# Mixing each tile with four row-tiled products on TensorE instead of one product with a masked block matrix

## The chip, the cores and the metric

The kernel runs on one core of one Trainium2 chip. Its metric is the device time of one execution in microseconds, the median of several executions. A profile is one further execution; its span runs from the first to the last instruction and is shorter than its time, which also has what lies around the instructions.

## The reference

`x` has 64 batches of 32 channels by 512 features. Two layers are applied and the result is added to `x`:

```python
W = weights[condition]                       # (64, 32, 32), one of 16 matrices for each batch
y = einsum('bct,bcd->bdt', x, W)             # mixes the 32 channels of a batch
result = einsum('bnd,od->bno', y, W_base) + b_base
logits = einsum('bnd,ed->bne', y, W_gate)    # 8 experts
route_w = top-2 of softmax(logits), divided by their sum, 0 elsewhere
h = einsum('bnd,erd->bner', y, A)            # rank 16 for each expert
delta = einsum('bner,eor->bno', h * route_w[..., None], B)
out = x + result + delta
```

All of it is float32. The large products are done as three products of values split into a high and a low part (`hi*hi + hi*lo + lo*hi`, type float32r); the mixing is a plain float32 product.

## The kernel before

**Tiles.** A tile is four batches (Q = 4), 4 x 32 channels on the 128 partitions, by 512 features; there are 16 tiles. `x_sb[:, t, :]` holds tile t, `mixw[:, t, :]` the four 32x32 mixing matrices of its batches, one below the other (partition = batch in tile x 32 + channel). The first two tiles' matrices are picked out of a table by TensorE, the other 14 are gathered by indirect DMAs of GpSimd.

**Mixing.** VectorE (`select`, L366) multiplies `mixw` with a mask, `diag_mask`, so that a 128x128 block-diagonal matrix `mix[t % 2]` arises. TensorE (`mix_tile`, L508) then makes y transposed, features on the partitions: for each of 4 chunks of 128 features one product with `x_sb[:, t, chunk]` (128x128) as the stationary operand and `mix` (128 columns) as the moving one, into one PSUM bank `y_ps[t % 2]`. A float32 product is two pairs of weight load and matmul in the trace, so a tile has 8 pairs. Tile 0's second half goes into another bank (`hwT_ps[0]`), so that its first half can be read early.

**The rest of a tile.** ScalarE makes `y_hi` (`split_y`, L287) and VectorE `y_lo` (`low_y`, L382), both two-buffered. TensorE's `main_step` (L521) runs 12 steps (4 chunks, 3 products of split values), two matmuls each, into the two banks of `main_ps[t % 2]`: base sums, LoRA ranks and gate logits. VectorE routes (`route_tile`: the top two, weights, `hw`), TensorE transposes `hw` (`turn`, L531) into the bank `hwT_ps[t % 2]`, ScalarE and VectorE split it (`split_hwT` L298, `low_hwT` L416), and `lora` (L537) adds six matmuls to the base sums. VectorE adds the bias and the sums to x (`add_bias` L423, `finish` L427), and SyncE stores.

**Order.** TensorE's order is written out by hand. In the iteration of tile t: `mix_tile(t + 1)`, four main steps of t, `turn(t - 1)`, five main steps, `lora(t - 1)`, three main steps. `mix_tile(t + 1)` waits for `mix` and for `y_lo(t - 1)`, since `y_ps` has two buffers. In the iteration of tile 1 the mixing of tile 2 comes after four main steps. In the opening, `mix_tile(0)` and `mix_tile(1)` come directly one after the other, then the main steps of tile 0 in the order of `FIRST_ORDER`, each waiting for its chunk of W to be landed and split (`split_w` L281, `low_w` L372). The last two tiles have an order of their own (L597, L603, L636).

**VectorE's order** in an iteration: `route_tile(t - 1)`, `select(t + 2)`, `low_hwT(t - 1)`, `low_y(t + 1)`, `add_bias`, `finish(t - 1)`. GpSimd's gathers and SyncE's loads of x for later tiles wait for `y_done`.

PSUM's eight banks: `y_ps` 2, `main_ps` 2 x 2, `hwT_ps` 2.

Of the kernel before, what the change touches and what calls it, by code (L numbers as in the profile page):

```python
# [5 lines left out]
def adaln_ffn_kernel(  # L6
# [7 lines left out]
    out: bass.AP,  # L14
):


# [4 lines left out]
    f32 = mybir.dt.float32  # L22
# [31 lines left out]
    TURN_AT, LORA_AT = 4, 9  # L54
    SECOND_MIX_AT = 4

# [17 lines left out]
    with ctx:  # L74
        def sb(name, shape, dt=f32):
            return ctx.enter_context(nc.sbuf_tensor(name, shape, dt))

        def ps(name):
            return ctx.enter_context(nc.psum_tensor(name, [P, 512], f32))

        def sem(name):
            return ctx.enter_context(nc.semaphore(name))
# [11 lines left out]
        ident = sb("ident", [P, P])  # L94
        diag_mask = sb("diag_mask", [P, Q, C])
        channel = sb("channel", [P, 1], i32)
# [14 lines left out]
        mixw = sb("mixw", [P, TILES, C])  # L111
        mix = [sb(f"mix{i}", [P, Q, C]) for i in range(2)]

# [13 lines left out]

        y_ps = [ps(f"y_ps{i}") for i in range(2)]
        main_ps = [ctx.enter_context(nc.psum_tensor(f"main_ps{i}", [P, 2, 512], f32)) for i in range(2)]
        hwT_ps = [ps(f"hwT_ps{i}") for i in range(2)]  # L130


# [14 lines left out]
        cleared = sem("cleared")  # L147
        mask_cleared = sem("mask_cleared")
        mask_ready = sem("mask_ready")
        experts_ready = sem("experts_ready")  # L150
# [6 lines left out]
        rows_ready = sem("rows_ready")  # L157
        mix_ready = sem("mix_ready")
        xb_ready = sem("xb_ready")
# [3 lines left out]
        b_lo_ready = sem("b_lo_ready")  # L163
        first_y_done = sem("first_y_done")
        first_y_hi_ready = sem("first_y_hi_ready")
# [30 lines left out]

        def first_halves():

            for h, bank in enumerate((y_ps[0], hwT_ps[0])):
                f = slice(h * D // 2, (h + 1) * D // 2)  # L200
                yield bank[:, 0:D // 2], y_hi[0][:, f], y_lo[0][:, f]

# [74 lines left out]
        @block.scalar  # L277
        def _(act):
            def split_w(c):
                act.wait_ge(w_landed[c], 16)  # L280
                act.activation(w_hi[:, c, :], w_raw[:, c, :], ACT.Copy).then_inc(w_hi_ready, 1)  # L281

            def split_y(t):
                act.wait_ge(y_done, t + 1)
                if t >= 2:
                    act.wait_ge(main_done, t - 1)
                act.activation(y_hi[t % 2][:, :], y_ps[t % 2][:, :], ACT.Copy).then_inc(y_hi_ready, 1)  # L287

            def exp_second(t):
                act.wait_ge(top_ready, t + 1)  # L290
                act.activation(second[:, :], top[:, 0:1], ACT.Exp, bias=top[:, 1:2], scale=-1.0)\  # L291
                    .then_inc(second_ready, 1)

            def split_hwT(t):
                act.wait_ge(hwT_done, t + 1)
                if t >= 2:
                    act.wait_ge(base_done, t - 1)
                act.activation(hwT_hi[t % 2][:, :], hwT_ps[t % 2][:, 0:P], ACT.Copy)\  # L298
                    .then_inc(hwT_hi_ready, 1)

            act.dma_start(table[:, 0, :, :], cond_w.rearrange("(p k) d -> p k d", k=K)).then_inc(table_landed, 16)
            split_w(0)
            for (y, hi, _), done, ready in zip(first_halves(), (first_y_done, y_done),
                                               (first_y_hi_ready, y_hi_ready)):
                act.wait_ge(done, 1)
                act.activation(hi, y, ACT.Copy).then_inc(ready, 1)
            split_w(1)
            split_w(2)
            split_w(3)
            split_y(1)  # L310
            act.wait_ge(b_landed, 16)
            act.activation(b_hi[:, :], b_raw[:, :], ACT.Copy).then_inc(b_hi_ready, 1)
# [12 lines left out]
        def _(dve):  # L325
            dve.memset(diag_mask[:, :, :], 0.0).then_inc(mask_cleared, 1)
            dve.wait_ge(mask_cleared, 1)
            for q in range(Q):
                last = dve.memset(diag_mask[q * C:(q + 1) * C, q, :], 1.0)
            last.then_inc(mask_ready, 1)  # L330


# [22 lines left out]
            def select(t):  # L355
                if t < PICKED:
                    dve.wait_ge(picked, t + 1)
                    dve.tensor_reduce(mixw[:, t, :], picked_ps[t].rearrange("p s d -> p d s"), AXIS.X, ALU.add)\
                        .then_inc(first_mixw_ready, 1)
                    dve.wait_ge(first_mixw_ready, t + 1)  # L360
                    dve.wait_ge(mask_ready, 1)
                else:
                    dve.wait_ge(mixw_landed[t - PICKED], 16)
                if t >= 2:
                    dve.wait_ge(y_done, t - 1)
                dve.tensor_tensor(mix[t % 2][:, :, :],  # L366
                                  mixw[:, t, :].unsqueeze(1).to_broadcast([P, Q, C]),
                                  diag_mask[:, :, :], ALU.mult).then_inc(mix_ready, 1)

# [10 lines left out]
            def low_y(t):  # L380
                dve.wait_ge(y_hi_ready, t + 1)
                dve.tensor_tensor(y_lo[t % 2][:, :], y_ps[t % 2][:, :], y_hi[t % 2][:, :].bitcast(f32),  # L382
                                  ALU.subtract).then_inc(y_lo_ready, 1)
# [30 lines left out]
            def low_hwT(t):  # L414
                dve.wait_ge(hwT_hi_ready, t + 1)
                dve.tensor_tensor(hwT_lo[t % 2][:, :], hwT_ps[t % 2][:, 0:P], hwT_hi[t % 2][:, :].bitcast(f32),  # L416
                                  ALU.subtract).then_inc(hwT_lo_ready, 1)
# [17 lines left out]
            low_w(0)  # L435
            for (y, hi, lo), have, ready in zip(first_halves(), (first_y_hi_ready, y_hi_ready),
                                                (first_y_lo_ready, y_lo_ready)):
                dve.wait_ge(have, 1)
                dve.tensor_tensor(lo, y, hi.bitcast(f32), ALU.subtract).then_inc(ready, 1)
            low_w(1)  # L440
            low_w(2)
            low_w(3)
            low_y(1)
            select(2)
            dve.wait_ge(experts_ready, 1)
# [5 lines left out]
            for t in range(1, LAST):  # L451
                before = main_ps[(t - 1) % 2]
                route_tile(t - 1, before[:, :, BASE:HALF], before[:, 1, HALF:HALF + E])
                if t == 1:
                    low_b()
                if t + 2 < TILES:
                    select(t + 2)
                if t < LAST - 1:
# [34 lines left out]
        def _(pe):  # L493
            def warm_up(columns):
                for n in columns:
                    pe.matmul(hwT_ps[1][:, 0:n], ones[:, 0:P], ones[:, 0:n], start=True, stop=True)  # L496

            def mix_tile(t):
                pe.wait_ge(mix_ready, t + 1)
                pe.wait_ge(x_landed[t], 16)  # L500
                if t >= 2:
                    pe.wait_ge(y_lo_ready, t - 1)
                for c in range(CHUNKS):
                    f = slice(c * P, (c + 1) * P)
                    dst = y_ps[t % 2][:, f]
                    if t == 0 and c >= CHUNKS // 2:
                        dst = hwT_ps[0][:, (c - CHUNKS // 2) * P:(c - CHUNKS // 2 + 1) * P]
                    last = pe.matmul(dst, x_sb[:, t, f], mix[t % 2][:, :, :], start=True, stop=True)  # L508
                    if t == 0 and c == CHUNKS // 2 - 1:
                        last.then_inc(first_y_done, 1)  # L510
                last.then_inc(y_done, 1)
# [162 lines left out]
```

## Time and profile before

| | |
|---|---|
| time, median of 3 runs | 95.22 us (95.0 to 95.29) |
| the profiled execution's own time | 95.87 us |
| its span | 94.0 us |
| PE busy | 90.2 us (96%) |
| PE weight load busy | 86.6 us (92%) |
| VectorE busy | 65.3 us (69%) |
| ScalarE busy | 23.5 us (25%) |
| GpSimd busy | 16.2 us (17%) |
| mean granted TensorE clock | 1.000 |

Busy shares are means over the whole span. A matmul's duration in the rows is that of one matmul from its start to its modelled end, and successive ones overlap; how fast they follow is read from the distance of their starts. PE is TensorE's matmuls, PEld its weight loads.

### The profile page before, as it was taken

The numbers are of one execution on the slowest core, as the hardware profiler recorded it, in microseconds if no ns is written. First come the engines' busy times: TensorE is split into PE (matmuls) and PEld (weight loads), VectorE is DVE, ScalarE is ACT, GpSimd is POOL, SyncE is SP. The second block draws the span as 40 slices with busy tenths as digits, with TensorE's granted clock in tenths as the row PEclk, the third lists the DMA queues.
The fourth block names the chain that finished last, engine by engine and source line by source line (L and its number), as shares of the span: only waits on it lengthen the run. The fifth ranks groups of instructions, "written<-read, shape, count | busy, mean of one in ns | idle before, by whom it ended". The sixth has DMA issues, their size and how long they took to land.

```text
span 94.0 us, 1811 instructions
## 1 busy us (share of the span) xinstructions
PE 90.2 (96%) x643; PEld 86.6 (92%) x643; DVE 65.3 (69%) x228; ACT 23.5 (25%) x55; POOL 16.2 (17%) x29
## 2 busy tenths in 40 slices
PE   6998999999999999999999999999999999999980
PEld 2397899999999999999999999999999999999970
DVE  2884997867575866867575866777575968867660
ACT  4065813311304031311304031311304031311210
POOL 5158404120404040120404040120400000000000
PEclk9999999999999999999999999999999999999999
DMA  1999163340607042330507061330606020302023
GB/s 38 292 319 369 59 192 142 112 121 34 196 0 222 8 163 74 124 106 36 194 0 224 13 192 38 125 108 37 194 9 222 1 112 0 112 7 112 0 112 112
DMA packets 6360, 10.65 MB, mean 113 GB/s; under 512 B 1008, under 2 KB 1616, under 8 KB 6352
## 3 DMA queue, kind: packets, MB, share of 16 engines
q1 hardware_dynamic: 5616, 10.12, 33.0%
q0 software_dynamic: 448, 0.23, 1.0%
q10 hardware_dynamic: 288, 0.20, 0.7%
q8 instruction: 5, 0.08, 0.4%
q14 instruction: 3, 0.02, 0.1%
HBM read 6.35 MB, written 4.19 MB: 112 GB/s over the span
## 4 chain that ended last, share of the span: by engine, by line
PE 87%; DMA 6%; SPq 2%; DVE 1%; ACT 1%; issue 0%
PE main_ps L521 53%; PE y_ps L508 13%; PE main_ps L537 11%; DMA w_raw<-w_all 6%; PE main_ps L597 5%; PE main_ps L603 3%; PE hwT_ps L531 2%; SPq L208 1%; DVE x_sb L489 1%; ACT w_hi L281 1%; SPq L211 0%; SPq L213 0%; PE main_ps L636 0%
## 5 line engine op out<-in xcount | busy, mean ns | idle before, releaser
L521 PE MATMUL main_ps<-w_hi,y_hi 128*128 128x320 f32 x112 | 27.1, 322 | 0.4 <-ACT w_hi L281 0.4
L521 PE MATMUL main_ps<-w_lo,y_hi 128*128 128x320 f32 x112 | 26.9, 321 | 0.0
L521 PE MATMUL main_ps<-w_hi,y_lo 128*128 128x320 f32 x112 | 25.8, 312 | 0.0
L258 POOL DMA_INDIRECT mixw<-cond_w,row_ids x14 | 14.0, 1002 | 48.7 <-PE y_ps L508 46.2
L521 PEld LDWEIGHTS main_ps<-w_hi,y_lo 128*128 128x128 f32 x112 | 19.0, 188 | 0.0
L521 PEld LDWEIGHTS main_ps<-w_hi,y_hi 128*128 128x128 f32 x112 | 18.0, 190 | 0.9 <-ACT w_hi L281 0.9
L521 PEld LDWEIGHTS main_ps<-w_lo,y_hi 128*128 128x128 f32 x112 | 18.5, 189 | 0.1
L508 PE MATMUL y_ps<-mix,x_sb 128*128 128x128 f32 x124 | 16.9, 279 | 0.0
L508 PEld LDWEIGHTS y_ps<-mix,x_sb 128*128 128x128 f32 x124 | 16.0, 195 | 0.1
L291 ACT ACTIVATE second<-top 128x1 f32<-128x1 f32 x16 | 4.7, 296 | 42.7 <-DVE top L389 42.7
L427 DVE TENSOR_TENSOR x_sb<-main_ps,x_sb 128x512 f32<-128x512 f32 x15 | 10.3, 690 | 4.8 <-PE main_ps L537 4.7
L416 DVE TENSOR_TENSOR hwT_lo<-hwT_ps,hwT_hi 128x128 fp32r<-128x128 f32 x16 | 4.7, 292 | 12.9 <-ACT hwT_hi L298 12.9
L423 DVE TENSOR_TENSOR x_sb<-x_sb,bias_sb 128x512 f32<-128x512 f32 x16 | 10.8, 682 | 0.0
L287 ACT ACTIVATE y_hi<-y_ps 128x512 fp32r<-128x512 f32 x15 | 9.0, 598 | 6.5 <-PE y_ps L508 6.5
L382 DVE TENSOR_TENSOR y_lo<-y_ps,y_hi 128x512 fp32r<-128x512 f32 x15 | 10.2, 681 | 0.1
L298 ACT ACTIVATE hwT_hi<-hwT_ps 128x128 fp32r<-128x128 f32 x16 | 4.4, 277 | 12.1 <-PE hwT_ps L531 12.1
L537 PE MATMUL main_ps<-b_hi,hwT_lo 128*128 128x256 f32 x30 | 6.0, 284 | 0.0
L407 DVE SCALAR_TENSOR_TENSOR hw<-main_ps,weight,route 128x128 f32<-128x128 f32 x16 | 5.6, 351 | 0.6
L537 PE MATMUL main_ps<-b_lo,hwT_hi 128*128 128x256 f32 x30 | 6.0, 282 | 0.0
L537 PE MATMUL main_ps<-b_hi,hwT_hi 128*128 128x256 f32 x30 | 6.0, 282 | 0.0
L537 PEld LDWEIGHTS main_ps<-b_hi,hwT_hi 128*128 128x128 f32 x30 | 5.1, 189 | 0.0
L496 PE MATMUL hwT_ps<-const-bfloat16-1.0 128*128 128x512 bf16 (+1 forms) x10 | 4.3, 556 | 0.8 <-PEq L667 0.8
(66 smaller groups left out, 87.0 us busy)
## 6 DMA issues: line engine op xcount, KB each, us to landing
x_sb<-x SPq DMA_DIRECT2D x16, 256.0 KB, 3.1
out<-x_sb SPq DMA_DIRECT2D x15, 256.0 KB, 2.1
w_raw<-w_all SPq DMA_DIRECT2D x4, 324.0 KB, 5.6
b_raw<-b_lora SPq DMA_DIRECT2D x1, 256.0 KB, 6.3
bias_sb<-bias SPq DMA_DIRECT2D x1, 256.0 KB, 4.4
mixw<-cond_w,row_ids POOLq DMA_INDIRECT x14, 2.7
out<-x_sb ACTq DMA_DIRECT2D x1, 128.0 KB, 1.8
out<-x_sb SPq DMA_DIRECT2D x1, 128.0 KB, 1.8
```

The costliest lines, as they stand in the source:

```text
L258: pool.indirect_dma_start(mixw[:, t, :], None, cond_w, bass.IndirectOffsetOnAxis(row_ids[:, t:t + 1], 0))\
L287: act.activation(y_hi[t % 2][:, :], y_ps[t % 2][:, :], ACT.Copy).then_inc(y_hi_ready, 1)
L291: act.activation(second[:, :], top[:, 0:1], ACT.Exp, bias=top[:, 1:2], scale=-1.0)\
L382: dve.tensor_tensor(y_lo[t % 2][:, :], y_ps[t % 2][:, :], y_hi[t % 2][:, :].bitcast(f32), ALU.subtract).then_inc(y_lo_ready, 1)
L407: dve.scalar_tensor_tensor(out=hw[t % 2][:, :].rearrange("p (h e r) -> p h e r", h=2, e=G), in0=h.rearrange("p h (e r) -> p h e r", e=G), ...
L416: dve.tensor_tensor(hwT_lo[t % 2][:, :], hwT_ps[t % 2][:, 0:P], hwT_hi[t % 2][:, :].bitcast(f32), ALU.subtract).then_inc(hwT_lo_ready, 1)
L423: dve.tensor_tensor(x_sb[:, t, :], x_sb[:, t, :], bias_sb[:, :], ALU.add).then_inc(xb_ready, 1)
L427: dve.tensor_tensor(tile, sums, tile, ALU.add).then_inc(result_ready, 1)
L508: last = pe.matmul(dst, x_sb[:, t, f], mix[t % 2][:, :, :], start=True, stop=True)
L521: last = pe.matmul(main_ps[t % 2][:, half, 0:n_cols], y, w[:, half * HALF:half * HALF + n_cols], start=i == 0, stop=i == STEPS - 1)
L537: last = pe.matmul(sums[half], h[t % 2][:, :], w[:, half * BASE:(half + 1) * BASE], start=False, stop=n == 2, skip_group_check=True)
L597: last = pe.matmul(side_sums(t), y, w[:, BASE:ALL], start=i == 0, stop=i == STEPS - 1)
```

## The change

`mix_tile` makes, for each chunk of 128 features, four products, one for each batch q: stationary operand `x_sb` of the 32 partitions of q (32 x 128 features), moving operand `mixw` of the same 32 partitions (32 columns), in TensorE's row tile at row 32q, into columns of PSUM bank q. The four banks `y_ps[:, 0..3, :]` hold one tile's y; there is no second buffer, so `mix_tile(t)` waits for `y_lo(t - 1)` where it waited for `y_lo(t - 2)`. `diag_mask`, `mix` and VectorE's multiplication with the mask are gone. `y_hi` and `y_lo` are read out of the four banks by an access pattern of runs of 32. In the opening, `mix_tile(1)` stands after three main steps of tile 0, and tile 0's halves of y are handed on only when all of it is made. `hw` is transposed into unused columns of the first bank of `main_ps[t % 2]` (for the last two tiles into `y_ps`), as `hwT_ps` is gone.

```diff
-    SECOND_MIX_AT = 4
+    NEXT_MIX_AT, SECOND_MIX_AT = 3, 4
-        mix = [sb(f"mix{i}", [P, Q, C]) for i in range(2)]
-        y_ps = [ps(f"y_ps{i}") for i in range(2)]
+        y_ps = ctx.enter_context(nc.psum_tensor("y_ps", [P, Q, 512], f32))
-        hwT_ps = [ps(f"hwT_ps{i}") for i in range(2)]
+        def mixed(chunks):
+            return y_ps[:, :, chunks.start * C:chunks.stop * C].rearrange("p q (c d) -> p c q d", d=C)
+        def split(of, chunks):
+            return of[:, chunks.start * P:chunks.stop * P].rearrange("p (c q d) -> p c q d", q=Q, d=C)
+        def turned(t):
+            if t >= TAIL[0]:
+                return y_ps[:, t - TAIL[0], 0:P]
+            return main_ps[t % 2][:, 0, 512 - P:512]
...
-                act.activation(y_hi[t % 2][:, :], y_ps[t % 2][:, :], ACT.Copy).then_inc(y_hi_ready, 1)
+                act.activation(split(y_hi[t % 2], WHOLE), mixed(WHOLE), ACT.Copy).then_inc(y_hi_ready, 1)
...
-                act.activation(hwT_hi[t % 2][:, :], hwT_ps[t % 2][:, 0:P], ACT.Copy)\
+                act.activation(hwT_hi[t % 2][:, :], turned(t), ACT.Copy)\
...
-            for (y, hi, _), done, ready in zip(first_halves(), (first_y_done, y_done),
-                                               (first_y_hi_ready, y_hi_ready)):
-                act.wait_ge(done, 1)
-                act.activation(hi, y, ACT.Copy).then_inc(ready, 1)
+            act.wait_ge(y_done, 1)
+            for half, ready in ((FIRST_HALF, first_y_hi_ready), (SECOND_HALF, y_hi_ready)):
+                act.activation(split(y_hi[0], half), mixed(half), ACT.Copy).then_inc(ready, 1)
...
-                if t >= 2:
-                    dve.wait_ge(y_done, t - 1)
-                dve.tensor_tensor(mix[t % 2][:, :, :],
-                                  mixw[:, t, :].unsqueeze(1).to_broadcast([P, Q, C]),
-                                  diag_mask[:, :, :], ALU.mult).then_inc(mix_ready, 1)
...
-                dve.tensor_tensor(y_lo[t % 2][:, :], y_ps[t % 2][:, :], y_hi[t % 2][:, :].bitcast(f32),
+                dve.tensor_tensor(split(y_lo[t % 2], WHOLE), mixed(WHOLE), split(y_hi[t % 2], WHOLE).bitcast(f32),
                                   ALU.subtract).then_inc(y_lo_ready, 1)
...
-            for (y, hi, lo), have, ready in zip(first_halves(), (first_y_hi_ready, y_hi_ready),
-                                                (first_y_lo_ready, y_lo_ready)):
-                dve.wait_ge(have, 1)
-                dve.tensor_tensor(lo, y, hi.bitcast(f32), ALU.subtract).then_inc(ready, 1)
+            dve.wait_ge(y_hi_ready, 1)
+            for half, ready in ((FIRST_HALF, first_y_lo_ready), (SECOND_HALF, y_lo_ready)):
+                dve.tensor_tensor(split(y_lo[0], half), mixed(half), split(y_hi[0], half).bitcast(f32),
+                                  ALU.subtract).then_inc(ready, 1)
...
-                if t + 2 < TILES:
-                    select(t + 2)
...
             def mix_tile(t):
-                pe.wait_ge(mix_ready, t + 1)
+                if t < PICKED:
+                    pe.wait_ge(first_mixw_ready, t + 1)
+                else:
+                    pe.wait_ge(mixw_landed[t - PICKED], 16)
                 pe.wait_ge(x_landed[t], 16)
-                if t >= 2:
-                    pe.wait_ge(y_lo_ready, t - 1)
+                if t >= 1:
+                    pe.wait_ge(y_lo_ready, t)
                 for c in range(CHUNKS):
-                    f = slice(c * P, (c + 1) * P)
-                    dst = y_ps[t % 2][:, f]
-                    if t == 0 and c >= CHUNKS // 2:
-                        dst = hwT_ps[0][:, (c - CHUNKS // 2) * P:(c - CHUNKS // 2 + 1) * P]
-                    last = pe.matmul(dst, x_sb[:, t, f], mix[t % 2][:, :, :], start=True, stop=True)
+                    for q in range(Q):
+                        rows = slice(q * C, (q + 1) * C)
+                        last = pe.matmul(y_ps[:, q, c * C:(c + 1) * C], x_sb[rows, t, c * P:(c + 1) * P],
+                                         mixw[rows, t, :], start=True, stop=True, tile_position=(q * C, 0))
                 last.then_inc(y_done, 1)
...
-                pe.transpose(hwT_ps[t % 2][:, 0:P], hw[t % 2][:, :], ident[:, :]).then_inc(hwT_done, 1)
+                pe.matmul(turned(t), hw[t % 2][:, :], ident[:, :], is_transpose=True, start=t >= TAIL[0], stop=True,
+                          skip_group_check=True).then_inc(hwT_done, 1)
...
             mix_tile(0)
-            mix_tile(1)
 
             for i, (c, n) in enumerate(FIRST_ORDER):
+                if i == NEXT_MIX_AT:
+                    mix_tile(1)
```

## Rows read from the trace of the kernel before

**Rows 1.** The page's chain that ended last, by engine and by line
```profile
PE 87%; DMA 6%; SPq 2%; DVE 1%; ACT 1%; issue 0%
PE main_ps L521 53%; PE y_ps L508 13%; PE main_ps L537 11%; DMA w_raw<-w_all 6%; PE main_ps L597 5%; PE main_ps L603 3%; PE hwT_ps L531 2%; SPq L208 1%; DVE x_sb L489 1%; ACT w_hi L281 1%; SPq L211 0%; SPq L213 0%; PE main_ps L636 0%
```
**Rows 2.** That chain in order of time: start us, us, what
```profile
9.66 3.54 PE main_ps L521 x22
13.19 0.89 PE y_ps L508 x8
...
43.73 0.89 PE y_ps L508 x8
44.62 1.19 PE main_ps L521 x8
45.80 0.11 PE hwT_ps L531
45.91 1.49 PE main_ps L521 x10
47.41 0.71 PE main_ps L537 x6
48.12 0.90 PE main_ps L521 x6
...
80.73 0.89 PE y_ps L508 x8
```
**Rows 3.** Groups of instructions by line and form, page's columns (busy us, mean ns)
```profile
L508 PE MATMUL y_ps<-mix,x_sb 128*128 128x128 f32 x124 | 16.9, 279 | 0.0
L366 DVE TENSOR_TENSOR mix<-mixw,diag_mask 128x128 f32<-128x128 f32 x16 | 4.5, 283 | 0.1
```
**Rows 4.** Timeline of PE and weight loads around one mixing: start us, us, engine
```profile
43.27 0.46 PE L521 MATMUL main_ps<-w_hi,y_lo 128*128 128x320 f32 x2
43.42 1.01 PEld L508 LDWEIGHTS y_ps<-mix,x_sb 128*128 128x128 f32 x8
43.57 1.05 PE L508 MATMUL y_ps<-mix,x_sb 128*128 128x128 f32 x8
```
**Rows 5.** PE after a wait, and before it: the same columns
```profile
9.34 0.31 PE L521 MATMUL main_ps<-w_hi,y_lo 128*128 128x328 f32 x1
9.66 0.42 PE L521 MATMUL main_ps<-w_hi,y_hi 128*128 128x320 f32 x1
```
**Rows 6.** Weight loads of two lines: duration ns min/median/max, first and last start
```profile
L508 PEld LDWEIGHTS y_ps<-mix,x_sb x124: 187/192/338, 5.1 to 81.2; 128*128 128x128 f32 x124
L531 PEld LDWEIGHTS hwT_ps<-ident,hw x16: 137/138/147, 13.8 to 89.6; 128*128 128x128 f32 x16
```
**Rows 7.** Timeline of all engines in the same iteration: VectorE and ScalarE
```profile
41.18 0.68 DVE L382 TENSOR_TENSOR y_lo<-y_ps,y_hi 128x512 fp32r<-128x512 f32 x1
42.87 0.69 DVE L427 TENSOR_TENSOR x_sb<-main_ps,x_sb 128x512 f32<-128x512 f32 x1 [0.41 <-PE main_ps L537]
44.66 0.60 ACT L287 ACTIVATE y_hi<-y_ps 128x512 fp32r<-128x512 f32 x1 [0.39 <-PE y_ps L508]
44.80 0.35 DVE L407 SCALAR_TENSOR_TENSOR hw<-main_ps,weight,route 128x128 f32<-128x128 f32 x1
44.89 0.94 POOL L258 DMA_INDIRECT mixw<-cond_w,row_ids  x1 [4.34 <-PE y_ps L508]
```
**Rows 8.** Timeline of the opening
```profile
5.08 1.09 PE L508 MATMUL y_ps<-mix,x_sb 128*128 128x128 f32 x4
...
6.21 0.38 ACT L306 ACTIVATE y_hi<-y_ps 128x256 fp32r<-128x256 f32 x1 [0.21 <-PE y_ps L508]
6.45 1.06 PE L508 MATMUL y_ps<-mix,x_sb 128*128 128x128 f32 x8
7.11 0.41 DVE L439 TENSOR_TENSOR y_lo<-hwT_ps,y_hi 128x256 fp32r<-128x256 f32 x1
8.79 0.57 PE L521 MATMUL main_ps<-w_hi,y_hi 128*128 128x320 f32 x2 [0.37 <-ACT w_hi L281]
```

More of the change, by code:

```diff
@@ L76, in sb @@
             return ctx.enter_context(nc.sbuf_tensor(name, shape, dt))
-        def ps(name):
-            return ctx.enter_context(nc.psum_tensor(name, [P, 512], f32))
         def sem(name):
@@ L94, in adaln_ffn_kernel @@
         ident = sb("ident", [P, P])
-        diag_mask = sb("diag_mask", [P, Q, C])
         channel = sb("channel", [P, 1], i32)
@@ L147, in adaln_ffn_kernel @@
         cleared = sem("cleared")
-        mask_cleared = sem("mask_cleared")
-        mask_ready = sem("mask_ready")
         experts_ready = sem("experts_ready")
@@ L157, in adaln_ffn_kernel @@
         rows_ready = sem("rows_ready")
-        mix_ready = sem("mix_ready")
         xb_ready = sem("xb_ready")
@@ L163, in adaln_ffn_kernel @@
         b_lo_ready = sem("b_lo_ready")
-        first_y_done = sem("first_y_done")
         first_y_hi_ready = sem("first_y_hi_ready")
@@ L195, in two_runs @@
             return bass.AP(first.tensor, first.offset, [first.ap[0], [step, 2], [1, count]])
[L197 to L201, printed above, removed]
+        def mixed(chunks):
+            return y_ps[:, :, chunks.start * C:chunks.stop * C].rearrange("p q (c d) -> p c q d", d=C)
+        def split(of, chunks):
+            return of[:, chunks.start * P:chunks.stop * P].rearrange("p (c q d) -> p c q d", q=Q, d=C)
+        WHOLE, FIRST_HALF, SECOND_HALF = (slice(*bounds) for bounds in
+                                          ((0, CHUNKS), (0, CHUNKS // 2), (CHUNKS // 2, CHUNKS)))
+        def turned(t):
+            if t >= TAIL[0]:
+                return y_ps[:, t - TAIL[0], 0:P]
+            return main_ps[t % 2][:, 0, 512 - P:512]
         block = ctx.enter_context(nc.Block())
@@ L325, in _ @@
         def _(dve):
[L326 to L330, printed above, removed]
             dve.wait_ge(cond_landed, 16)
@@ L355, in select @@
             def select(t):
[L356 to L363, printed above, removed]
-                if t >= 2:
-                    dve.wait_ge(y_done, t - 1)
-                dve.tensor_tensor(mix[t % 2][:, :, :],
-                                  mixw[:, t, :].unsqueeze(1).to_broadcast([P, Q, C]),
-                                  diag_mask[:, :, :], ALU.mult).then_inc(mix_ready, 1)
+                dve.wait_ge(picked, t + 1)
+                dve.tensor_reduce(mixw[:, t, :], picked_ps[t].rearrange("p s d -> p d s"), AXIS.X, ALU.add)\
+                    .then_inc(first_mixw_ready, 1)
             def low_w(c):
@@ L415, in low_hwT @@
                 dve.wait_ge(hwT_hi_ready, t + 1)
-                dve.tensor_tensor(hwT_lo[t % 2][:, :], hwT_ps[t % 2][:, 0:P], hwT_hi[t % 2][:, :].bitcast(f32),
+                dve.tensor_tensor(hwT_lo[t % 2][:, :], turned(t), hwT_hi[t % 2][:, :].bitcast(f32),
                                   ALU.subtract).then_inc(hwT_lo_ready, 1)
@@ L443, in _ @@
             low_y(1)
-            select(2)
             dve.wait_ge(experts_ready, 1)
@@ L495, in warm_up @@
                 for n in columns:
-                    pe.matmul(hwT_ps[1][:, 0:n], ones[:, 0:P], ones[:, 0:n], start=True, stop=True)
+                    pe.matmul(y_ps[:, Q - 1, 0:n], ones[:, 0:P], ones[:, 0:n], start=True, stop=True)
             def mix_tile(t):
-                pe.wait_ge(mix_ready, t + 1)
+                if t < PICKED:
+                    pe.wait_ge(first_mixw_ready, t + 1)
+                else:
+                    pe.wait_ge(mixw_landed[t - PICKED], 16)
                 pe.wait_ge(x_landed[t], 16)
-                if t >= 2:
-                    pe.wait_ge(y_lo_ready, t - 1)
+                if t >= 1:
+                    pe.wait_ge(y_lo_ready, t)
                 for c in range(CHUNKS):
-                    f = slice(c * P, (c + 1) * P)
-                    dst = y_ps[t % 2][:, f]
-                    if t == 0 and c >= CHUNKS // 2:
-                        dst = hwT_ps[0][:, (c - CHUNKS // 2) * P:(c - CHUNKS // 2 + 1) * P]
-                    last = pe.matmul(dst, x_sb[:, t, f], mix[t % 2][:, :, :], start=True, stop=True)
-                    if t == 0 and c == CHUNKS // 2 - 1:
-                        last.then_inc(first_y_done, 1)
+                    for q in range(Q):
+                        rows = slice(q * C, (q + 1) * C)
+                        last = pe.matmul(y_ps[:, q, c * C:(c + 1) * C], x_sb[rows, t, c * P:(c + 1) * P],
+                                         mixw[rows, t, :], start=True, stop=True, tile_position=(q * C, 0))
                 last.then_inc(y_done, 1)
```

## The prediction

> **What bounds the kernel now.** I read the page's chain that ended last first, to see whose work sets the end, then the same chain in order of time, to see where each mixing lies on it, and then timelines around one mixing. The chain is TensorE for 87% of the span, and the mixing line L508 has 13% of it [rows 1]. In order of time [rows 2], nothing but PE follows once it starts at 9.66 us: an iteration is 0.89 (mixing) + 1.19 + 0.11 (turn) + 1.49 + 0.71 (lora) + 0.90 = 5.29 us with no gap. The mixings on that chain are those of tiles 2 to 15, 14 pieces of 0.89 us, the first at 13.19 and the last at 80.73. Those of tiles 0 and 1 lie before 8.79, where PE waits for a chunk of W [rows 8]; they cost nothing as long as they end in time. So each us that a mixing takes more or less counts 14 times at the end, and what VectorE and ScalarE do counts only where it makes PE wait.
>
> **How fast a mixing pair can go.** A tile has 8 pairs of load and matmul in 0.89 us, 0.112 us a pair [rows 2]. The reader should see in [rows 4] that both engines are full: the first of the eight loads starts at 43.42, when the second of the two matmuls before starts, and its own matmul only at 43.57. A load runs one matmul ahead, never two. How long does a load occupy the array? After a wait, when no load could be done ahead, the same kind of matmul lasts 0.42 instead of 0.31 us [rows 5]: 0.11 us of load stand open. The loads of float32 values last 192 ns by the median, those of the turn, of the same size but in transpose mode, 138 [rows 6], so the load of a turn is some 0.05 us cheaper. I take 0.107 us for a mixing load, nearly the whole of a pair's 0.112. The mixing of before is then bound by its matmuls and by its loads at once.
>
> **The products themselves.** The change makes 16 products for a tile where there were 4, so 32 pairs for 8. Moving columns: 32 x 32 against 8 x 128, the same number, and up to four times fewer in a row if four row tiles run at the same time. But each of the 32 loads still brings in 128 columns of x; only its rows are fewer. By the Trainium skill ("TensorE: Matmul & The Clock Gate", LDWEIGHTS (loading the stationary operand)) the time of a load goes by its columns and not by its rows, 107 ns for 128 columns. The trace has no load of 32 rows; its 128-row loads agree with that figure where they stand open [rows 5].
>
> So the mixing becomes bound by loads, and the question is how many of them go on at once. No row shows a row tile. Three ways: all 32 one after the other, 32 x 0.112 = 3.58 us; four at once throughout, 8 x 0.112 = 0.90 us; or what I hold likeliest, overlap between row tiles but not within one. A product's two pairs are neighbours in the order and use the same row tile. The second load can start only when the first matmul has taken its weights, as a load is never two matmuls ahead [rows 4], and the next product's matmul is queued behind the second one. Then each of the 16 products holds one open load, 16 x 0.112 = 1.79 us, and the load of the next row tile lies under it.
>
> **The changes of form.** Each mixing now stands between full-array products and back. From below: the turn is also of another form (transpose mode), and takes 0.11 us for 128 columns, with nothing beside it [rows 2]; so nothing. From above: the array empties and loads anew at both ends. A mixing matmul lasts 0.279 us in the mean [rows 3] against 0.112 a pair, so 0.17 us to empty, and 0.11 for the open load [rows 5]: 0.28 each time, 0.56 a tile, 14 x 0.56 = 7.8 us. I take one open load a tile, 0.11, as at 9.66, the nearest row. The Trainium skill speaks against the change here: by "TensorEngine Tiling (Array Packing)", Key Properties, a change of tiling mode drains TensorE. By that rule the sum would have the upper bound in place of the 0.11, some 6.3 us more; no run here shows it yet.
>
> A mixing: 1.79 + 0.11 = 1.90 us, 1.01 more than 0.89; 14 of them, 14.1 us.
>
> **The mask and VectorE.** 16 multiplications of 0.283 us go [rows 3]. In the iterations they are off the chain: PE never waits for VectorE there. What hides them is that the turn has room: `hw` is made at 44.80 + 0.35 = 45.15, and the turn's piece begins at 45.80 [rows 2, 7]. Nothing is gained, and nothing lost if that cover goes, as the work itself goes. In the opening, one multiplication starts mixing 0 some 0.29 us earlier, at 4.79.
>
> **One buffer for y.** `mix_tile(t + 1)` now waits for `y_lo(t)`. That is made from 41.18 to 41.86 and mixing starts at 43.57 [rows 4, 7]: 1.7 us of room. Behind the wait stand the mixing and all of the main steps; GpSimd's gather (it idles 4.34 us before each, [rows 7]) and SyncE's loads of x wait for `y_done` behind it, with an iteration or more to spare. The cost is nothing. The room stays, as y_hi starts when the mixing ends and the time from there to the next mixing, 1.19 + 0.11 + 1.49 + 0.71 + 0.90 = 4.40 us, is unchanged. Reading y out of four banks in runs of 32 may cost ScalarE (0.60) and VectorE (0.68) [rows 7] nothing or, if they doubled, 1.3 us; both are within the 1.7 us: nothing on the chain.
>
> **The transposed ranks.** The turn has the same size and the same place. Its bank belongs to the other buffer of the sums than the one PE is writing, and lora, which writes it next, waits for `hwT_lo` already. Nothing. `finish` ends at 43.56 and the main steps that wait for it start at 44.62 [rows 2, 7]: a mixing shorter than 0.89 would still leave room, and a longer one leaves more.
>
> **The opening.** Here the longer mixings come out of cover. Until 5.9 us, mixing pairs start some 0.21 us apart (four matmuls in 1.09 us from 5.08, where later eight take 1.06) [rows 8]. From 4.79, 5 of the 16 products pass by 5.9 and 11 more take 1.23 us: 7.1, and 0.2 until the result is seen, 7.3. ScalarE's two halves (0.38 each) end at 8.1, VectorE's two (0.41 each), now behind both, at 8.95. Only then may mixing 1 start: 8.95 + 1.90 = 10.85. The two steps (1,0) and (1,2) follow, four matmuls of 0.149 (1.49 us for ten, [rows 2]), 0.60 us, and the dense part starts at 11.45 instead of 9.66: 1.8 us. If a mixing took 0.90, it would be 4.79 to 6.3, halves at 7.1 and 8.05, mixing 1 until 8.95, and the dense part at 9.66 as now: nothing.
>
> **The sum.** 14.1 + 1.8 = 15.9 us. On the profiled execution's own time, 94.0 of span and 1.87 around it: 111.8. The median of the runs is 0.65 us below that execution: 111.1 us.
>
> **The rivals.** (a) *Four loads at once.* A mixing takes 0.90 us, plus 0 to 0.56 for the changes of form: 14 x 0.01 to 0.57, 95.3 to 103.2, about 97 with one open load a tile. For it: the columns streamed fall to a quarter, and loads of different rows need nothing of each other. Against: the two pairs of a product share a row tile. The Trainium skill stands on its side ("TensorEngine Tiling (Array Packing)", Key Properties: different tiles can execute their loads and matmuls in parallel). (b) *Faster: a load of 32 rows occupies its tile for less than the 0.107 us of a full one.* If it takes what a turn's does, 0.107 - 0.054 = 0.053, and four go at once, a mixing takes 8 x 0.053 + 0.11 = 0.53, 14 x -0.36 = -5.0 us: 90.2 us. It decides from the point where a mixing falls below 0.89 us, so where a load costs under 0.10 us at four at once, or under 0.05 at overlap of neighbours. Against it are the two loads of the same size in [rows 6] with 192 ns; for it that no row shows a load of fewer rows. With changes of form at half of their bound it gives 92 to 93. (c) *All loads one after the other.* 3.58 + 0.11 a mixing, 14 x 2.80 = 39.2, and over 5 in the opening: 139 us. Against it: loads and matmuls overlap in every row of the trace. (d) *The change does not do what it says:* the row tiles run, but y's single buffer makes PE wait. It needs y_lo to be 1.7 us later; then each us beyond costs 14. I give it little.
>
> **How the numbers follow.** Forecast (one open load for each product) 0.38, its own range 108 to 117 (no cost of changes, to the full bound). (a) 0.25, of which 0.05 is within 0.3%. (b) 0.25. (c) 0.07, (d) and others 0.05, mostly slower. A measurement of this kernel can tell from no change what is over 0.3%, about 0.3 us. Faster: 0.25; within: 0.06; slower: 0.69. The range leaves out (c), the upper end of the forecast with a full drain and the lowest part of (b): 90.5 to 116.
>
> **What the profile after would show.** Right: pieces of L508 on the chain of about 1.9 us, 32 loads each, with starts of every second load 0.11 us apart and no row of PE waiting for VectorE within the iterations; iterations of 6.3 us; the dense part from about 11.4 us. Wrong: mixing pieces of 0.9 or less (four at once), load durations well below 190 ns (cheap loads), PE idle before L508 with y_lo named (d), or a gap at each border of a mixing much above 0.11 us.

## The result, and the profile after

The changed kernel takes 104.97 us (median of 4, 104.76 to 105.06) against 95.25 us for the kernel before: a ratio of 1.1007, interval 1.0974 to 1.104. It is slower, as forecast, and within the stated range, but by 9.7 us and not by 15.9. The span of the profiled execution is 103.0 us, 9.0 more than before; most of the other 0.7 us comes from which executions were profiled: the one of the kernel before took 95.87 us, 0.62 above its median, and that of the changed kernel 104.76, 0.21 below its own. The executions of one kernel differ mostly in their opening, in some of the variants below by several us, and there the pieces of the chain decide and not the medians.

Its page has the chain by engine and line, and the slices of the span with the granted clock, in tenths of full speed:

```profile
PE   6937999999999999999999999999999999999990
PEclk9995559999999999999999999999999999999999
...
PE 89%; DMA 4%; another core or an unknown queue 1%; ACT 1%; SPq 1%; DVE 1%; issue 1%
PE main_ps L506 53%; PE y_ps L494 16%; PE main_ps L524 10%; PE main_ps L585 5%; DMA w_raw<-w_all 4%; PE main_ps L591 3%; PE main_ps L517 2%; DVE x_sb L474 1%; ACT w_hi L285 1%; SPq L212 0%; ACT y_hi L309 0%; SPq L217 0%; PE main_ps L624 0%; PE y_ps L517 0%
```

The bound is TensorE as before [rows 1]. The chain in order of time says where the 9 us are (L494 is the mixing, L506 the main steps, L517 the turn, L524 lora):

```profile
5.99 0.74 ACT w_hi L285
6.73 1.16 another core or an unknown queue
7.89 0.02 issue
7.92 0.39 ACT y_hi L309
8.31 0.14 issue
8.44 1.96 PE main_ps L506 x6
10.40 1.86 PE y_ps L494 x32
12.26 5.29 PE main_ps L506 x26
17.55 1.02 PE y_ps L494 x32
...
33.16 1.02 PE y_ps L494 x32
34.19 1.38 PE main_ps L506 x8
35.56 0.11 PE main_ps L517
35.67 1.49 PE main_ps L506 x10
37.16 0.71 PE main_ps L524 x6
...
89.30 1.02 PE y_ps L494 x32
```

A *visit* is one stretch of row-tiled products among full-array ones, with the way in and out; a *slot* is the 0.112 us in which one pair of load and matmul follows another. Set beside [rows 2], the chain gives two separate losses. **The opening:** tile 2 is mixed at 17.55 instead of 13.19, 4.36 us later. **The visits:** from there to the last mixing it is 71.75 us instead of 67.54, 4.21 more in 13 iterations, 0.324 each. The last visit and what follows add 0.43. Together 9.0.

In an iteration the mixing's piece has grown from 0.89 to 1.02, and the piece of eight matmuls behind it from 1.19 to 1.38; all other pieces are the same. So the loss of a visit is 0.13 + 0.19 us, and more than half of it shows on the matmuls *behind* the mixing. The timeline shows the borders (matmuls, then weight loads):

```profile
43.93 0.46 PE L506 MATMUL main_ps<-w_hi,y_lo 128*128 128x320 f32 x2
44.32 1.09 PE L494 MATMUL y_ps<-mixw,x_sb 32*128 32x32 f32 x32
45.34 0.56 PE L506 MATMUL main_ps<-w_hi,y_hi 128*128 128x320 f32 x2
...
44.32 0.98 PEld L494 LDWEIGHTS y_ps<-mixw,x_sb 32*128 32x128 f32 x32 [0.20 <-issue]
45.34 0.30 PEld L506 LDWEIGHTS main_ps<-w_hi,y_hi 128*128 128x128 f32 x2
```

In [rows 4] the loads led their matmuls by one, across both borders. Now the first load starts at 44.32 with its own matmul, 0.20 us after loading had stopped, and so does the first load behind, at 45.34. Nothing is loaded ahead across a change of form. That the 32 pairs between the borders take what 8 took is what `e3` below shows.

### The profile page after: what moved, and what is told of

Its sections match the earlier page's. It is cut to its first block, busy times and chain, and to the rows that moved or that the text cites. A ratio compares the mean times of both kernels' runs of the same rounds, so it can differ in the third digit from the quotient of the medians.

```text
span 103.0 us, 2542 instructions
## 1 busy us (share of the span) xinstructions
PE 97.2 (94%) x1027; PEld 90.2 (88%) x1027; DVE 61.3 (60%) x207; ACT 23.1 (22%) x55; POOL 15.6 (15%) x29
## 4 chain that ended last, share of the span: by engine, by line
PE 89%; DMA 4%; another core or an unknown queue 1%; ACT 1%; SPq 1%; DVE 1%; issue 1%
PE main_ps L506 53%; PE y_ps L494 16%; PE main_ps L524 10%; PE main_ps L585 5%; DMA w_raw<-w_all 4%; PE main_ps L591 3%; PE main_ps L517 2%; DVE x_sb L474 1%; ACT w_hi L285 1%; SPq L212 0%; ACT y_hi L309 0%; SPq L217 0%; PE main_ps L624 0%; PE y_ps L517 0%
## 5 line engine op out<-in xcount | busy, mean ns | idle before, releaser
L506 PE MATMUL main_ps<-w_hi,y_hi 128*128 128x320 f32 x112 | 28.1, 333 | 2.4 <-ACT y_hi L309 2.4
L506 PE MATMUL main_ps<-w_lo,y_hi 128*128 128x320 f32 x112 | 27.5, 327 | 0.0
L506 PE MATMUL main_ps<-w_hi,y_lo 128*128 128x320 f32 x112 | 26.5, 319 | 0.0
L506 PEld LDWEIGHTS main_ps<-w_hi,y_hi 128*128 128x128 f32 x112 | 18.6, 196 | 3.0 <-issue 2.5
L506 PEld LDWEIGHTS main_ps<-w_hi,y_lo 128*128 128x128 f32 x112 | 19.8, 195 | 0.0
L494 PEld LDWEIGHTS y_ps<-mixw,x_sb 32*128 32x128 f32 x512 | 16.5, 194 | 3.2 <-issue 3.1
L506 PEld LDWEIGHTS main_ps<-w_lo,y_hi 128*128 128x128 f32 x112 | 19.1, 195 | 0.1
L494 PE MATMUL y_ps<-mixw,x_sb 32*128 32x32 f32 x512 | 18.3, 281 | 0.0
L403 DVE TENSOR_TENSOR hwT_lo<-main_ps,hwT_hi 128x128 fp32r<-128x128 f32 x14 | 4.1, 292 | 18.5 <-ACT hwT_hi L302 18.5
L414 DVE TENSOR_TENSOR x_sb<-main_ps,x_sb 128x512 f32<-128x512 f32 x15 | 10.3, 690 | 4.8 <-PE main_ps L524 4.7
L302 ACT ACTIVATE hwT_hi<-main_ps 128x128 fp32r<-128x128 f32 x14 | 3.9, 277 | 11.1 <-PE main_ps L517 10.2
L524 PE MATMUL main_ps<-b_hi,hwT_lo 128*128 128x256 f32 x30 | 6.0, 283 | 0.0
L524 PE MATMUL main_ps<-b_lo,hwT_hi 128*128 128x256 f32 x30 | 6.0, 282 | 0.0
L524 PE MATMUL main_ps<-b_hi,hwT_hi 128*128 128x256 f32 x30 | 6.0, 281 | 0.0
L376 DVE MAX8 top<-main_ps 128x8 f32<-128x8 f32 x16 | 2.8, 174 | 5.3 <-PE main_ps L506 5.1
L524 PEld LDWEIGHTS main_ps<-b_hi,hwT_hi 128*128 128x128 f32 x30 | 5.1, 188 | 0.0
```

The costliest lines, as they stand in the source:

```text
L403: dve.tensor_tensor(hwT_lo[t % 2][:, :], turned(t), hwT_hi[t % 2][:, :].bitcast(f32), ALU.subtract).then_inc(hwT_lo_ready, 1)
L414: dve.tensor_tensor(tile, sums, tile, ALU.add).then_inc(result_ready, 1)
L494: last = pe.matmul(y_ps[:, q, c * C:(c + 1) * C], x_sb[rows, t, c * P:(c + 1) * P], mixw[rows, t, :], start=True, stop=True, tile_position ...
L506: last = pe.matmul(main_ps[t % 2][:, half, 0:n_cols], y, w[:, half * HALF:half * HALF + n_cols], start=i == 0, stop=i == STEPS - 1)
L524: last = pe.matmul(sums[half], h[t % 2][:, :], w[:, half * BASE:(half + 1) * BASE], start=False, stop=n == 2, skip_group_check=True)
```

## The experiments

Each kernel is the changed one with the edit shown, except where it says "before"; the edits are cut to their main lines. Pieces of the chain are those of an iteration in the middle, and the other mixings of that kernel at the same clock are like them to 0.01 us.

**The visit: borders or products?** `e3` makes the products twice in a row, `e4` cuts the mixing in two visits.

```diff
+                for again in range(2 if t >= 2 else 1):
                     for c in range(CHUNKS):
```


> The changed kernel with the 16 products of each mixing from tile 2 on made twice in a row, 14 tiles. Theory A (a mixing is 8 slots of 0.112 us and a fixed cost of 0.33 at its borders, which is paid once a visit): 14 x 0.90 = 12.5 us more, 117.5 us. Theory B (the row tiles are slower throughout, 1.22 us for 16 products): 14 x 1.22 = 17.1 us more, 122.1 us.

```diff
                 for i, (c, n) in enumerate(ORDER):
...
                     main_step(t, i, c, n)
+                    if t > 1 and i == 0:
+                        mix_part(t + 1, range(CHUNKS // 2, CHUNKS))
```


> The changed kernel with the mixing of 12 tiles (3 to 14) cut in two: chunks 0 and 1 at its place, chunks 2 and 3 behind the first main step; no product more or less. Theory A (each change between full-array and row-tiled products costs, 0.33 us a visit): 12 x 0.33 = 4.0 us more, 109.0 us. Theory B (the 0.33 us belong to the products or to a wait ahead of the mixing, not to the borders): 105.0 us.

`e3` took 115.84 us (112.65 to 117.61), `e4` 106.81 (104.47 to 109.06). The chains, `e3` first:

```profile
42.70 1.92 PE y_ps L495 x64
```
```profile
43.15 0.58 PE y_ps L497 x16
43.73 0.49 PE main_ps L510 x2
44.22 0.58 PE y_ps L497 x16
44.80 1.09 PE main_ps L510 x6
```

Twice the products in one visit: 1.92 for 1.02, 0.90 more, theory A to the hundredth. The same products in two visits: 0.58 + 0.49 + 0.58 + 1.09 = 2.74 for 1.02 + 1.38 = 2.40, 0.34 more. So a mixing is 0.90 us of products and some 0.33 us for going in and out, of which the old 0.89 had none. The medians agree with that less well, +10.9 for 12.5 and +1.8 for 4.0, and the openings are the reason. Counted from the mixing of tile 2 to the end, the profiles have 97.9 us (`e3`, from 17.91) and 89.4 (`e4`, from 14.98) against 85.45 (from 17.55): +12.4 and +4.0, what theory A asks for.

**The border without the rest of the change.** Into the kernel before, one extra product ahead of each mixing: row-tiled, or full-array as the control.

```diff
+                if t >= 2:
+                    pe.matmul(y_ps[t % 2][:, 0:C], x_sb[0:C, t, 0:P], mix[t % 2][0:C, 0, :],
+                              start=True, stop=True, tile_position=(0, 0))
```


> The kernel before with one more product in front of each mixing from tile 2 on (14 of them): 32 x 128 stationary in a row tile, 32 moving columns; its result is overwritten by the mixing. Theory A (changing to a row tile and back costs about 0.33 us wherever it is done, beside 2 slots of 0.112): 14 x 0.55 = 7.7 us more, 103 us. Theory B (no cost of the change of form): 14 x 0.22 = 3.1 us more, 98.4 us.

```diff
+                if t >= 2:
+                    pe.matmul(y_ps[t % 2][:, 0:C], x_sb[:, t, 0:P], mix[t % 2][:, 0, :], start=True, stop=True)
```


> The control for the row-tiled extra product: the kernel before with one more product in front of each mixing from tile 2 on, 128 x 128 stationary over the full array, 32 moving columns. Both theories: 2 slots of 0.112 us, 14 x 0.22 = 3.1 us more, 98.4 us. The distance of the two is the cost of the change of form: 4.6 us by theory A, none by theory B.

102.88 us (102.81 to 103.02) and 98.59 us (98.15 to 98.69), 95.5 for the kernel before beside them. Their distance is 4.3 us, 0.31 for each of 14. The chains (`e7`, then `e8`) have it in the two pieces, 0.33 + 1.09 against 0.14 + 0.97:

```profile
40.80 0.33 PE y_ps L504 x2
41.14 1.09 PE y_ps L511 x8
```
```profile
44.51 0.14 PE y_ps L504 x2
44.65 0.97 PE y_ps L510 x8
```

This is the cleanest comparison, as nothing else of the change is in either kernel: a single row-tiled product among full-array ones costs 0.31 us more than the same count of pairs without a change of form. The Trainium skill ("TensorEngine Tiling (Array Packing)", Key Properties) says that a change of tiling mode drains TensorE. The runs agree as far as they can show it: in and out cost 0.31 to 0.34 us together, and no load is made ahead.

**What a slot is made of.** Half as many stationary columns, or half as many moving ones. `e5` leaves out half of the mixed features, `e6` half of the mixed channels. In both, the idle products ahead of the mixing of tile 0 also go into all four banks of `y_ps` in turn and not into the last one alone.

```diff
-                        last = pe.matmul(y_ps[:, q, c * C:(c + 1) * C], x_sb[rows, t, c * P:(c + 1) * P],
+                        last = pe.matmul(y_ps[0:P // 2, q, c * C:(c + 1) * C], x_sb[rows, t, c * P:c * P + P // 2],
                                          mixw[rows, t, :], start=True, stop=True, tile_position=(q * C, 0))
```


> The changed kernel with stationary operands of 64 columns instead of 128 in the mixing: only the first 64 features of each chunk are made, the others keep stale values. Same number of products, same moving columns. Theory A (the slot of 0.112 us is the load, which goes by its columns): slots of about 0.06 us, 14 x 8 x -0.05 = -6 us, about 99 us. Theory B (a fixed time for a pair, or the moving columns): 105.0 us.

```diff
-                        last = pe.matmul(y_ps[:, q, c * C:(c + 1) * C], x_sb[rows, t, c * P:(c + 1) * P],
-                                         mixw[rows, t, :], start=True, stop=True, tile_position=(q * C, 0))
+                        last = pe.matmul(y_ps[:, q, c * C:c * C + C // 2], x_sb[rows, t, c * P:(c + 1) * P],
+                                         mixw[rows, t, 0:C // 2], start=True, stop=True, tile_position=(q * C, 0))
```


> The changed kernel with 16 moving columns instead of 32 in each product of the mixing: half of the mixed channels are made, the others keep stale values. Same loads. Theory A (bound by loads): 105.0 us. Theory B (bound by the moving columns, in that the four row tiles' columns go one after the other): 4 x 0.027 = 0.107 us a slot halves, -6 us, about 99 us.

93.84 us and 102.98 us. The chain has 0.60 and 1.01 us for a mixing (`e5` first):

```profile
42.34 0.60 PE y_ps L494 x32
42.94 1.38 PE main_ps L506 x8
```
```profile
42.86 1.01 PE y_ps L494 x32
```

The moving columns do nothing (1.01 for 1.02), the loaded columns do it: 0.42 us less for eight slots, 0.052 a slot, half of the 0.107 that the prediction took for a full load. Fewer loaded columns also means fewer results, but `e6` makes just as few and gains nothing, so it is not the results. The loads themselves last 187 ns by the median with 128 columns and 133 with 64; the lines of the mixing's loads (duration ns min/median/max), the changed kernel's first and then `e5`'s:

```profile
L494 PEld LDWEIGHTS y_ps<-mixw,x_sb x512: 181/187/333, 5.0 to 90.0; 32*128 32x128 f32 x171
```
```profile
L494 PEld LDWEIGHTS y_ps<-mixw,x_sb x512: 127/133/133, 5.0 to 79.0; 32*64 32x64 f32 x171
```

Of `e5`'s 11.1 us, 14 x 0.42 = 5.9 are this; the rest is its opening, which mixes tile 2 at 12.45 instead of 17.55. `e6` is 2.0 us below the changed kernel although its mixings are the same, and 1.5 of them are its opening (tile 2 at 16.09). A load of 32 rows lasts what one of 128 rows lasts (187 against 192 ns, [rows 6]), and four at a time still take a slot of 0.112 us; so rival (b) is refuted.

**Which products run side by side?**

```diff
-                for c in range(CHUNKS):
-                    for q in range(Q):
+                for q in range(Q):
+                    for c in range(CHUNKS):
```


> The changed kernel with the loops of the mixing exchanged: all four chunks of one batch, then the next batch, so that neighbouring products use the same row tile. Theory A (each row tile works through its own pairs, whatever stands between them in the order): 105.0 us, no change. Theory B (products overlap only with their neighbours in the order): 32 pairs of 0.112 a tile for 8, 14 x 2.7 = 38 us more, about 143 us.

130.28 us (130.1 to 130.4). Neither theory. Its chain, and its slices of the granted clock:

```profile
41.55 2.42 PE y_ps L494 x32
```
```profile
PEclk9975569995999999997799999999999999999999
```

The mixing takes 2.42 us, between 1.02 and 3.6. In the trace, each batch's eight pairs follow at 0.112 us, and the next batch's first load starts 0.47 us after that of the batch before, four slots and not eight: 3 x 0.47 + 8 x 0.112 = 2.3. The first two stretches of 0.47 us have 5 loads, one batch's, and then 10, those of two batches (the mixing alone; the columns: us, busy of PE, of PEld, granted clock, DMA share, GB/s):

```profile
41.48:41.95 0.47, 0.47 (x4) 0.47 (x5) 1.00 0.00 0
41.95:42.42 0.47, 0.47 (x10) 0.47 (x10) 1.00 0.31 118
```

So the products need not be neighbours to overlap, but a row tile's work starts only about four pairs ahead of its turn. With the batches in the inner loop all four start together. The order of the loops is worth 14 x 1.40 = 19.6 us in the iterations. The opening has 2.65 more (tile 2 at 20.20), as the mixing of tile 1, at the lower clock, takes 4.48 us for 1.86. The remaining 3.1 of the 25.3 go with the granted clock, which fell again near 28 and 59 us: it reads 0.53 from 28.4 to 32.0 us, and PE was busy all the time from 26.0 on.

**The opening.** Ten, or five, idle products behind the mixing of tile 0; and an opening as before with row tiles from tile 2 on.

```diff
             mix_tile(0)
+            for _ in range(10):
+                pe.matmul(main_ps[1][:, 1, :], ones[:, 0:P], ones[:, 0:512], start=True, stop=True)
```


> The changed kernel with ten idle bf16 products of 512 columns right behind the mixing of tile 0, where TensorE stands idle from 6.0 to 8.4 us. Theory A (the opening's 4.4 us are for the larger part the clock, granted at half from the idle stretch on, over about 6.8 us): 101.5 us, 3.4 less than 105.0, with a granted clock of 1.0 behind 8.4 us. Theory B (the opening's loss is data that comes late and nothing else): 105.0, whatever the clock.

> The changed kernel with five idle products of 512 columns behind the mixing of tile 0 instead of ten. Theory A (any work there keeps the clock): 101.5 us as with ten. Theory B (the gap must be filled to its end): between 102 and 105.0 us, with half-rate starts of matmuls behind the gap.

```diff
-            mix_tile(0)
+            mix_full(0)
+            mix_full(1)
...
-                if i == NEXT_MIX_AT:
-                    mix_tile(1)
```


> Row-tiled mixing for tiles 2 to 15 only, as in the changed kernel; tiles 0 and 1 are mixed with the mask and full-array products as in the kernel before (tile 0's halves in two of the four banks, tile 1 in the third), and the second mixing follows the first directly. Theory A (the loss has two separate parts: 14 visits of 0.33 us, and the opening with row-tiled products): the mixing of tile 2 on the chain at about 13.2 us as before, 95.4 + 14 x 0.33 = 100.0 us. Theory B (the opening's delay comes from the rest of the change, such as the longer program or reading y out of four banks): about 104 to 105 us.

101.72 us with ten (101.46 to 102.03, and one execution at 104.02), 102.43 with five (101.98 to 103.46), 99.67 (99.24 to 100.04) with the old opening. Between ten and five the runs do not decide: the intervals of the two ratios overlap (1.0627 to 1.0684, 1.0652 to 1.078). In the profile with five, 103.46 us, PE idles 1.24 us and the clock is at the lower level from 10.3 to 13.7 us, as theory B of that run has it. What the clock did in the changed kernel, by windows (the columns: us, busy of PE, PEld, DVE, ACT, POOL, granted clock, DMA share, GB/s):

```profile
0.70:6.10 5.40, 5.29 (x51) 2.62 (x51) 2.31 (x8) 1.40 (x2) 2.41 (x9) 1.00 0.74 200
6.10:8.40 2.30, 0.00 (x0) 0.00 (x0) 0.83 (x1) 1.11 (x3) 1.64 (x5) 0.94 1.03 384
...
8.44:12.26 3.82, 3.82 (x39) 3.42 (x39) 2.98 (x5) 2.03 (x4) 0.00 (x0) 0.50 0.48 171
12.26:17.55 5.29, 5.29 (x31) 5.09 (x30) 1.66 (x9) 1.41 (x3) 0.97 (x1) 0.74 0.42 127
```

PE has no instruction for 2.3 us, and then works at a granted clock of 0.50, the lower of its two levels, 1.2 GHz. The clock costs 3.82 x 0.50 + 5.29 x 0.26 = 3.3 us. The ten products give back 3.25 and the mean granted clock is 1.00 in all five executions. The one that was profiled is the one at 104.02, though, and has the ten products themselves on the chain, for 3.43 us; from 11 us on its main matmuls follow at 0.15 us, the full rate. The opening of the others can't be seen.

The idle stretch is not all that the clock depends on. In `e6` ScalarE's `y_hi` starts at 6.23 and not at 7.92, PE idles only 0.6 us, is busy for 1.5 us more, and then has the lower clock all the same (the columns as above):

```profile
6.20:6.70 0.50, 0.00 (x0) 0.00 (x0) 0.38 (x1) 0.47 (x2) 0.21 (x1) 1.00 1.00 384
6.75:8.30 1.55, 1.54 (x22) 1.27 (x22) 1.06 (x3) 1.14 (x3) 1.31 (x4) 1.00 1.03 405
8.35:15.10 6.75, 6.75 (x45) 6.71 (x42) 3.09 (x7) 2.38 (x5) 1.59 (x1) 0.50 0.61 179
```

This gives an estimate of the parts. `e6` mixes tile 2 at 16.09, of which the clock has 6.75 x 0.50 = 3.4 us; without it, it would be about 12.7, no later than in the kernel before. The changed kernel's 17.55 is then about 12.7 + 3.3 of the clock + 1.7 of a `y_hi` that starts late.

The old opening gives back more, 5.3 us: it has neither the clock's loss nor the late `y_hi`, and mixes tile 2 at 12.37:

```profile
5.36 1.88 PE y_ps L520 x16
7.24 1.49 PE main_ps L548 x10
8.72 0.01 issue
8.74 3.63 PE main_ps L548 x22
12.37 1.02 PE y_ps L536 x32
```

99.67 is 4.35 us above the kernel before beside it (95.32, ratio 1.0453, 1.0423 to 1.0482), 14 x 0.31. So the account is, to some tenths of a us, 4.4 us for the visits and 5.3 for the new opening. The chains say 4.6 (from the mixing of tile 2 to the end, 85.4 us against 80.8 in the kernel before) and 5.2 (tile 2 at 12.37 against 17.55). `e12` takes back the row tiles of the opening together with its order (tile 1 mixed directly behind tile 0, tile 0's y handed on in halves), and so does not say which of the two matters.

**Smaller loads at once?** If loads bound a slot, they can be cut by column tiles: 64 or 32 features a product, in 2 or 4 column tiles beside the 4 row tiles, all of the features made.

```diff
-                    for q in range(Q):
+                    for m in range(0, P, 64):
+                        for q in range(Q):
...
+                            last = pe.matmul(y_ps[m:m + 64, q, c * C:(c + 1) * C],
+                                             x_sb[rows, t, c * P + m:c * P + m + 64], mixw[rows, t, :],
+                                             start=True, stop=True, tile_position=(q * C, m))
```


> The changed kernel with the ten idle products in the opening, and each product of the mixing cut into two column tiles: 32 rows x 64 columns stationary, at columns 0 and 64 of the array, 64 pairs a tile for 32. The half loads of before took 0.60 us on the chain for a mixing instead of 1.02. Theory A (column tiles load at the same time, as row tiles do): mixings of about 0.60 us, 14 x 0.42 = 5.9 us less than 101.7, 95.8 us, level with the kernel before. Theory B (the two halves of a row tile's load go one after the other): about 1.0 us a mixing, 101.7 us.

> The same with four column tiles of 32 columns, 128 pairs a tile. Theory A (loads at the same time, a slot by the columns of a load, about 0.03 us): mixings of 0.4 us, 93 us. Theory B (pairs start no closer than the 0.007 us seen between neighbours in different row tiles, 128 x 0.007 = 0.9 us): 101 to 102 us. Theory C (the halves of a row tile's load go one after the other): 101.7 us or more.

102.28 us (101.56 to 103.11) and 111.27 us (110.28 to 112.16). On the chain:

```profile
44.78 0.79 PE y_ps L495 x53
```
```profile
41.55 1.22 PE y_ps L495 x72
```

Both kernels have the ten idle products, too. Some of the pairs are missing from these counts (64 and 128 are made). Column tiles do load beside one another, but not for nothing: 0.79 us with 64 columns, between the 0.60 of theory A and the 1.02 of B, and 1.22 with 32. The 0.23 us that `e9` gains a visit are less than the 0.33 of the borders, and it lost them in its opening, where tile 2 is mixed at 19.10. `e10` loses more than 14 x 0.20 = 2.8 us: a few stretches of its main steps take 1.6 us more in all, mostly with PE waiting for nothing that the profile shows, and its opening is longer, too. The first mixing of both came in bursts with gaps of that kind, here that of `e9`:

```profile
4.93 1.02 PE L495 MATMUL y_ps<-mixw,x_sb 32*64 32x32 f32 x46
6.36 0.32 PE L495 MATMUL y_ps<-mixw,x_sb 32*64 32x32 f32 x4 [0.41 <-issue]
...
7.84 0.49 PE L495 MATMUL y_ps<-mixw,x_sb 32*64 32x32 f32 x9 [0.35 <-issue]
```

No version with row tiles that makes all of y beat the kernel before.

## Why the prediction was right in its sign and wrong in its mechanism

- **What bounds the kernel, and 14 mixings on the chain:** right; 13 iterations of 0.324 and the last visit.
- **A load goes by its 128 columns, about 0.107 us, and the mixing becomes bound by loads:** right (`e5`, `e6`). This is why up to four times less moving time gave nothing: in the kernel before, loads and matmuls filled a slot about equally, and the change took away only the matmuls.
- **"The next product's matmul is queued behind the second one", 16 open loads, 1.79 us:** wrong, and the step on which the forecast's size hung. The row tiles do not wait for one another in the inner order; four pairs start within 0.02 us, and a tile takes 8 slots, 0.90 us. Rival (a) is what came in the iterations, its products at 0.90 and its borders at 0.33 of its 0 to 0.56; its upper end, 103.2 us, was passed because it had put the opening at nothing. I had read in [rows 4] that a load is never two matmuls ahead, and carried it over from one array to four separate ones. The Trainium skill states what came ("TensorEngine Tiling (Array Packing)", Key Properties: tiles load and multiply in parallel), and it was given 0.25.
- **The changes of form, 0.11 us chosen between 0 and 0.56:** the bounds held, the size was off, 0.31 to 0.34 measured. The timeline has an open load at *both* borders, where I took one; that leaves about 0.1 us for emptying, an estimate (0.33 - 2 x 0.11).
- **Mask, one buffer for y, the ranks' place, the four-bank reads: nothing.** Right in the iterations. Their `y_hi` and `y_lo` last 0.60 and 0.68 us as in [rows 7], and PE waits for neither. In the opening the one buffer has a part in it: before, the mixing of tile 1 filled the time in which tile 0's `y_hi` was made, and now PE idles there.
- **The opening, 1.8 us from mixings of 1.9 us:** the place was right, the mechanism wrong. It measured 4.4. The mixings there took 8 slots like the others, that of tile 1 at the lower clock; what cost was a `y_hi` that starts 1.7 us late and the clock at 0.50, and the forecast had neither.
- **The sum:** 14.1 + 1.8 = 15.9 forecast; 4.6 + 4.4 = 9.0 measured between the spans. One term was 9.5 us too high and the other 2.6 too low, so it is luck that the total is nearer than its parts. The range reached from below rival (a) to above the forecast, so a time inside it says nothing for the forecast's mechanism.

**What stays open.** In the changed kernel the last product of tile 0's mixing is recorded before 6.1 us and ScalarE's `y_hi`, which waits for it, begins at 7.92; ScalarE had been free since 6.73. The chain calls the 1.16 us before it an unknown queue. `e11` has the same, `y_hi` at 7.93, although TensorE had gone on to the next products at 6.18: there the engine itself was not held up, only the signal came late. In `e9` and `e10` the products of that same mixing come in bursts until 8.3 or later; in `e1` to `e6`, row-tiled too, `y_hi` follows directly. So what it hangs on is not shown. Nor is it shown what makes the clock fall in the opening and in `e2`: PE had idled 2.3 us in the changed kernel, 0.6 in `e6` and `e4`, where it fell, and 0.7 in `e5`, where it did not. And the reading of the clock has a gap: in `e3` it is 1.00 from the start, while the main matmuls up to 16.4 us follow each other at 0.27 instead of 0.149 us, the rate that goes with 0.50 elsewhere. A reading of 1.00 in the opening is therefore worth checking by the distance of the starts.

## What to carry to other kernels

Before splitting a small product into row tiles, ask whether its slots are bound by the moving columns or by the weight loads: here the row tiles shared out the first and ran four of the second at once, and four times as many loads at four at once is no gain. Count the visits, too: in these runs each excursion into row tiles cost about 0.3 us in a full TensorE stream, so it must save more than that, or be made rarely and long. Where row tiles are used, put the row tile in the innermost loop. And read the opening by itself: about half of this loss lay there, in an idle TensorE and a lower clock that no count of products shows.

## What was not expected of the hardware

- The distance of starts in neighbouring row tiles is 0.007 us, but a row tile's work starts only some four pairs ahead of its turn (0.47 us apart in `e2`), which made the order of two loops worth 19.6 us.
- The granted clock fell to the lower level not only behind an idle stretch of 2.3 us but also in `e6` behind one of 0.6 us and 1.5 us of work, and in `e2` within a stretch that PE filled (0.53 from 28.4 to 32.0 us).
- Column tiles of float32 products cut a mixing from 1.02 to 0.79 us at 64 columns and lengthened it to 1.22 at 32. That with 128 pairs a tile the number of pairs costs more than their loads is likely, and not shown.
